# Thirty-two routed experts behind a cross attention: eight weight buffers instead of four, gate and up products in f16 halves instead of f32

## The reference

```python
x = x + xattn(layernorm(x), ctx)      # x: (4, 512, 512), ctx: (4, 1601, 512), 16 heads of 32
x = x + ffn(layernorm(x))             # 2048 tokens of 512
# ffn: router picks 4 of 32 experts a token, each expert takes at most C = 80 tokens
Xp = x[slots_token].reshape(E, C, d)
G = jnp.einsum('ecd,edi->eci', Xp, W_gate)          # 80x512 by 512x256
U = jnp.einsum('ecd,edi->eci', Xp, W_up)
Y = jnp.einsum('eci,eid->ecd', jax.nn.silu(G) * U, W_down)
Yf = Y.reshape(EC, d) * slots_w[:, None]
out = jnp.zeros((T, d), x.dtype).at[slots_token].add(Yf)
shared = jax.nn.silu(x @ shared_gate.T) * (x @ shared_up.T) @ shared_down.T
```

## Time and profile before

| | us |
|---|---|
| median of 3 runs | 1368.89 |
| the profiled execution | 1375.18 |
| its span, first to last instruction | 1373.3 |
| mean granted clock of TensorE | 0.964 |
| first part, until the second begins | 953.8 |
| first turn of gathered rows | 1152.15 |
| first scatter issued | 1165.01 |
| last scatter issued | 1366.42 |

### The profile page before, as it was taken

The page is one execution under the profiler, slowest core; times in us unless marked ns, Lnnn a source line. Parts: engine busy times, 40 slices in busy tenths (PEclk is TensorE's granted clock), DMA queues, the critical chain, the costliest instruction groups (busy, mean ns, idle before and its releaser), DMA issues. The chain is left out here.

```text
span 1373.3 us, 22309 instructions
## 1 busy us (share of the span) xinstructions
PE 1226.1 (89%) x9044; PEld 459.1 (33%) x9044; DVE 886.2 (65%) x1169; ACT 668.2 (49%) x910; POOL 184.1 (13%) x299
## 2 busy tenths in 40 slices
PE   4988999999899899989989998995798959989986
PEld 2542222444222245422224441221443423333332
DVE  6765878777587877767788766896667732222221
ACT  4546996345798534488853449882211101111111
POOL 0210000132000013200001320000200001333332
PEclk9999999999999999999999999997899989999997
DMA  7200000222000112200011122011620103989893
GB/s 276 88 23 17 2 2 10 83 70 70 24 1 1 58 41 64 93 1 1 2 69 32 62 77 94 9 55 44 257 100 3 39 1 108 308 281 321 278 289 76
DMA packets 38389, 117.82 MB, mean 86 GB/s; under 512 B 6544, under 2 KB 6800, under 8 KB 33040
## 3 DMA queue, kind: packets, MB, share of 16 engines
q1 hardware_dynamic: 33168, 105.60, 21.8%
q0 software_dynamic: 5120, 10.82, 3.7%
HBM read 95.67 MB, written 20.73 MB: 85 GB/s over the span
## 5 line engine op out<-in xcount | busy, mean ns | idle before, releaser
L567 ACT ACTIVATE work<-ps 128x1024 f32<-128x1024 f32 (+1 forms) x416 | 403.1, 1021 | 50.0 <-PE ps L1040 47.4
L1046 PE MATMUL ps<-work,vals 128*32 128x512 f32 (+2 forms) x1664 | 221.0, 604 | 1.1 <-ACT work L567 0.8
L863 PE MATMUL ps<-wts,work 128*128 128x512 f16 x864 | 203.1, 387 | 14.6 <-DVE work L596 14.6
L1040 PE MATMUL ps<-quer,keys 32*128 32x512 f16 x2496 | 171.8, 377 | 26.9 <-ACT work L567 9.3
L779 DVE TENSOR_TENSOR work<-work 128x2048 f32<-128x2048 f32 x64 | 146.6, 2291 | 5.9
L779 DVE TENSOR_TENSOR attn<-attn,work 128x2048 f32<-128x2048 f32 x64 | 146.6, 2290 | 5.3
L863 PE MATMUL ps<-wts,hl 128*128 128x512 f16 x480 | 116.6, 396 | 22.3 <-DVE hl L596 22.3
L863 PEld LDWEIGHTS ps<-wts,work 128*128 128x128 f16 x864 | 83.2, 99 | 115.1 <-DVE work L596 14.8
L1040 PEld LDWEIGHTS ps<-quer,keys 32*128 32x128 f16 x2496 | 46.2, 92 | 217.4 <-ACT work L567 192.0
L1816 PE MATMUL f_ps<-wring,xgt 128*80 128x512 f32 x256 | 116.5, 598 | 0.0
L1398 ACT ACTIVATE yf<-f_ps,wc 80x512 f32<-80x512 f32 x32 | 21.9, 683 | 174.7 <-PE f_ps L1831 168.2
(11 more groups left out here) (216 smaller groups left out, 1507.2 us busy)
## 6 DMA issues: line engine op xcount, KB each, us to landing
wring<-in_wx SPq DMA_DIRECT2D x32, 1536.0 KB, 8.1
raw<-in_ctx SPq DMA_DIRECT2D x52, 256.0 KB, 2.9
work<-in_x SPq DMA_DIRECT2D x4, 1024.0 KB, 5.4
table<-nums SPq DMA_DIRECT2D x16, 256.0 KB, 2.1
out<-x1s SPq DMA_DIRECT2D x16, 256.0 KB
work<-in_x SPq DMA_DIRECT2D x12, 256.0 KB, 4.3
x<-work SPq DMA_DIRECT2D x12, 256.0 KB, 2.0
x2t_rows<-nums SPq DMA_DIRECT2D x12, 256.0 KB, 2.4
```

What stands on the lines that cost most here:

```text
L567: act.activation(prob[0:rows, s % PROBS, 2 * half:2 * half + 2, :], ps[0:rows, 2 * pair:2 * pair + 2, :], ACT.Exp, scale=SCALE).then_inc(a ...
L863: mm = pe.matmul(out, lhs(a, c)[:, cols], wts[:, w, z, c * D:(c + 1) * D], start=(k == 0), stop=(k == len(steps) - 1))
L1040: mm = pe.matmul(ps[:, 2 * pair + h % 2, :], k[h * HD:(h + 1) * HD, :], q[h * HD:(h + 1) * HD, :], start=(e == 0), stop=(e == len(terms) - 1))
L1046: return pe.matmul(ps[h * HD:(h + 1) * HD, NUM, :], vals[a:z, ORDER[n], g * P + h * HD:g * P + (h + 1) * HD], prob[a:z, s % PROBS, h, :], ...
```

## The change

- `wring` has eight buffers of one expert's weights, spread over SBUF. Six are loaded early in the second part (experts 0, 1, 2, 4, 5, then 3), 7 and 6 during the shared expert. Gathered rows keep four buffers.
- The gate and up weights of an expert are split into f16 halves in `wsplit` (two buffers): ACT writes the high half (`weight_high`, 128x2048), DVE the low half (`weight_low`). The gathered rows are split too (`rows_high` on ACT, `rows_low` on DVE). `gate_up_rows` is then 12 f16 matmuls of 512 columns. The down product stays in f32. The copy of the turned hidden rows moves from DVE to ACT (`hidden_copy`), and the copy of the routing weight (`wc`) is gone.
- The loops of the experts are written out.
- To make room: `x2t` of batches 0 and 1 is loaded at the start of the second part, the residual rows of batches 0 to 2 share one buffer (`x1_block`), loaded batch after batch once the results of the one before are stored, and small tiles move.
- In the attention, `text_part` takes 128 columns in each of the steps 6 to 9 instead of 256 in steps 6 and 8.
- Several semaphores are merged (`d_link`, `p_link`), with the same number of waits.

```diff
 BIG = 1000.0
-RING = 4
+RING = 8
+GATHERS = 4
...
-        self.x2t = [at(f"x2t{i}", o * KB_, [P, QT, 2, NC, P], F16) for i, o in enumerate((8, 16, 48, 56))]
-        self.x1s = [at(f"x1s{i}", o * KB_, [P, 4, D], F32) for i, o in enumerate((74, 82, 90, 100))]
+        self.x2t = [at(f"x2t{i}", o * KB_, [P, QT, 2, NC, P], F16) for i, o in enumerate((48, 56, 64, 76))]
+        self.x1_last = at("x1_last", 8 * KB_, [P, QT, D], F32)
+        self.x1_block = at("x1_block", 190 * KB_, [P, QT, D], F32)
...
-        self.wring = at("wring", 132 * KB_, [P, RING, 3 * 2 * D], F32)
...
+        self.wring = [at(f"wring{i}", o * KB_, [P, 3 * 2 * D], F32)
+                      for i, o in enumerate((132, 144, 156, 168, 84, 96, 64, 48))]
+        self.wsplit = [at(f"wsplit{i}", (24 + 8 * i) * KB_, [P, 2, NC * D], F16) for i in range(2)]
...
-                for t in range(2):
-                    sp.wait_ge(f_wlo, 3 * p + 2 + t)
-                    load_turned(t)
-                sp.wait_ge(s_xt, 32 * (p + 1))
...
-                        if g > 0 and n in (6, 8):
+                        if g > 0 and 6 <= n < 10:
                             if n == 6:
                                 pe.wait_ge(a_sum, added(bb, g - 1, ADDS - 1))
-                            at = 0 if n == 6 else HALF
-                            mm = text_part(g - 1, at, at + HALF)
-                            if n == 8:
+                            at = (n - 6) * P
+                            mm = text_part(g - 1, at, at + P)
+                            if n == 9:
                                 mm.then_inc(a_den, 1)
...
+            def load_turned(b):
+                sp.dma_start(x2t[b][:, :, :, :, :].rearrange("p j a c k -> p j (a c k)"),
+                             x2_dram[b * L:(b + 1) * L, :].rearrange("(j p) n -> p j n", p=P)).then_inc(s_x2[min(b, 1)], 16)
+
+            def load_expert(n):
+                sp.dma_start(wring[n % RING][:, :], d["wx"][n]).then_inc(s_ring[n % RING], 16)
+
             sp.dma_start(x1t[:, :, :], d["x"][(B - 1) * L:B * L, :].rearrange("(j p) n -> p j n", p=P)).then_inc(s_xr, 16)
+            load_turned(0)
             sp.dma_start(rraw[:, :], d["rw"]).then_inc(s_r, 16)
             sp.dma_start(ebias[:, :], d["ebias"].partition_broadcast(P)).then_inc(s_r, 16)
-            sp.dma_start(x2t[2][:, :, :, :, :].rearrange("p j a c k -> p j (a c k)"),
-                         x2_dram[2 * L:3 * L, :].rearrange("(j p) n -> p j n", p=P)).then_inc(s_x2, 16)
-            for e in range(RING - 1):
-                sp.dma_start(wring[:, e, :], d["wx"][e]).then_inc(s_ring[e], 16)
+            load_turned(1)
+            load_turned(2)
+            for n in (0, 1, 2, 4, 5):
+                load_expert(n)
             sp.wait_ge(t_sel, NG)
-            sp.dma_start(wring[:, RING - 1, :], d["wx"][RING - 1]).then_inc(s_ring[RING - 1], 16)
+            load_expert(3)
             for j in range(QT):
                 sp.wait_ge(n_norm, j + 1)
                 sp.dma_start(table[(LB + j) * P:(LB + j + 1) * P, 0:D], xn[j]).then_inc(s_tab, 16)
-            for k in range(B - 1):
-                sp.dma_start(x1s[k][:, :, :], x1_dram[k * L:(k + 1) * L, :].rearrange("(j p) n -> p j n", p=P)).then_inc(
+
+            def load_rows(k):
+                upto(sp, s_o, 16 * QT * k)
+                sp.dma_start(x1b[:, :, :], x1_dram[k * L:(k + 1) * L, :].rearrange("(j p) n -> p j n", p=P)).then_inc(
                     s_xl, 16)
 
             def results(k):
                 for q in range(QT):
                     j = k * QT + q
                     sp.wait_ge(f_ac, j + 1)
-                    sp.dma_start(out[j * P:(j + 1) * P, :], x1s[k][:, q, :]).then_inc(s_o, 16)
-
+                    sp.dma_start(out[j * P:(j + 1) * P, :], (x1b if k < B - 1 else x1t)[:, q, :]).then_inc(s_o, 16)
+
+            load_rows(0)
             results(0)
+            load_rows(1)
             sp.wait_ge(e_wv, 1)
             sp.dma_start(table[0:T, D:TROW].rearrange("(j p) n -> p j n", p=P), rt[5][:, :, :]).then_inc(s_wt, 16)
             results(1)
+            load_rows(2)
+            sp.wait_ge(f_gu, 2 * NI)
+            load_expert(7)
+            sp.wait_ge(f_gu, 3 * NI)
+            load_expert(6)
+            results(2)
             sp.wait_ge(e_ar, 1)
             sp.dma_start(ia[:, :], arow_sb.rearrange("a (s e) -> a s e", e=E)).then_inc(s_ia, 16)
-            results(2)
             results(3)
-            with sp.Fori(0, E // RING - 1) as o:
-                for k in range(RING):
-                    sp.wait_ge(m_y, o * RING + k + 3)
-                    sp.dma_start(wring[:, k, :], d["wx"][bass.ds((o + 1) * RING + k, 1)].rearrange("a p n -> (a p) n")).then_inc(s_ring[k], 16)
+            for n in range(RING, E):
+                sp.wait_ge(m_y, n - RING + 1)
+                load_expert(n)
...
-            pool.wait_ge(f_gu, 2 * NI)
-
             def gather(n):
...
+                pool.indirect_dma_start(out=xg[n % GATHERS][:, :], out_offset=None, in_=table[:, :],
+                                        in_offset=bass.IndirectOffsetOnAxis(ap=idx[:, n:n + 1], axis=0)).then_inc(
+                    s_g[n % GATHERS], 16)
 
             def scatter(n):
...
+                pool.wait_ge(m_yf, n + 1)
+                pool.indirect_dma_start(out=out[:, :], out_offset=bass.IndirectOffsetOnAxis(ap=idx[:, n:n + 1], axis=0),
+                                        in_=yf[n % 2][:, :], in_offset=None, compute_op=ALU.add).then_inc(s_sc, 16)
+
+            for n in range(GATHERS):
                 gather(n)
             pool.wait_ge(s_o, 16 * NT)
-            for n in range(1, E + 1):
-                if n > 1:
-                    pool.wait_ge(s_sc, (n - 1) * 16)
+            for n in range(E):
+                upto(pool, s_sc, 16 * n)
                 scatter(n)
-                if n + RING <= E:
-
-                    pool.wait_ge(m_xt, n)
-                    pool.wait_ge(m_w, n + 1)
-                    gather(n + RING)
+                if n + GATHERS < E:
+                    gather(n + GATHERS)
...
-            def expert(n, u):
-                act.wait_ge(m_gu, n)
-                act.wait_ge(m_t, n)
-                act.activation(eg[:, :], ps[0:CAP, 7 if u % 2 == 0 else 0, 0:I], ACT.Tanh, scale=0.5).then_inc(m_e, 1)
-                act.wait_ge(m_y, n + 2)
-                act.wait_ge(m_w, n + 1)
-                if not isinstance(n, int):
-                    act.wait_ge(s_sc, n * 16 - 32)
-                act.activation(yf[u % 2][:, :], ps[0:CAP, 2 + u % 2, :], ACT.Copy, scale=wc[u][:, 0:1]).then_inc(m_yf, 1)
-
...
+            def weight_high(n):
+                act.wait_ge(s_ring[n % RING], 16 * (n // RING + 1))
+                if n < 2:
+                    act.wait_ge(f_gu, 4 * NI)
+                else:
+                    act.wait_ge(m_gu, n - 1)
+                act.activation(wsplit[n % 2][:, 0, :], wring[n % RING][:, 0:NC * D], ACT.Copy, scale=WS).then_inc(m_wh, 1)
+
+            def rows_high(n):
+                act.wait_ge(m_xt, n + 1)
+                upto(act, m_gu, n - 1)
+                act.copy(xgt[n % 2][:, 0, :, :].rearrange("p c s -> p (c s)"), ps[:, 6, 0:NC * CAP]).then_inc(m_xh, 1)
+
+            def expert_tanh(n):
+                act.wait_ge(m_gu, n + 1)
+                upto(act, m_h, n)
+                act.activation(eg[:, :], ps[0:CAP, 7 if n % 2 == 0 else 0, 0:I], ACT.Tanh, scale=0.5 / WS).then_inc(m_e, 1)
+
+            def hidden_copy(n):
+                act.wait_ge(m_ht, n + 1)
+                upto(act, m_y, n - 1)
+                act.copy(ht[n % 2][:, :, :].rearrange("p c s -> p (c s)"), ps[:, 1, 0:2 * CAP]).then_inc(m_hc, 1)
+
+            def weighted(n):
+                act.wait_ge(m_y, n + 1)
+                upto(act, s_sc, 16 * (n - 1))
+                act.activation(yf[n % 2][:, :], ps[0:CAP, 2 + n % 2, :], ACT.Copy,
+                               scale=xg[n % GATHERS][:, D + n:D + n + 1]).then_inc(m_yf, 1)
+
+            for n in range(2):
+                weight_high(n)
+            for n in range(2):
+                rows_high(n)
+            expert_tanh(0)
+            for n in range(E):
+                if n + 2 < E:
+                    weight_high(n + 2)
+                hidden_copy(n)
+                if n + 1 < E:
+                    expert_tanh(n + 1)
+                if n + 2 < E:
+                    rows_high(n + 2)
+                weighted(n)
...
-
-            def hidden(n, u):
-                gu = ps[0:CAP, 7 if u % 2 == 0 else 0, :]
-                dve.wait_ge(m_e, n)
-                dve.wait_ge(m_ht, n)
-                dve.scalar_tensor_tensor(hh[:, :], eg[:, :], 1.0, gu[:, 0:I], ALU.add, ALU.mult).then_inc(m_t, 1)
-                dve.wait_ge(m_t, n + 1)
-                dve.scalar_tensor_tensor(hh[:, :], hh[:, :], 0.5, gu[:, I:2 * I], ALU.mult, ALU.mult).then_inc(m_h, 1)
-                dve.wait_ge(m_ht, n + 1)
```

(61 more changed lines are left out.)

## The result

The changed kernel takes 1403.99 us in the median (four runs, 1400.33 to 1407.98), the kernel before 1368.64 us beside it (1367.94 to 1371.42): 1.0243 times as long, 95% interval 1.022 to 1.0266. It is 35 us slower, where 8 us less were forecast, and it lies above the range. The profiled execution took 1406.58 us, with a span of 1404.8 us.

A forecast was written before the change was run, and what follows sets the result against it. While loads run, POOL's serial chain of scatter, landing, next scatter was taken as the bound, PE close behind. Terms -1.4, -7.7, +4.6, -3.6 sum to -8.1 us from 1368.9: 1361 us, own range 1354 to 1367, 8-in-10 range 1347 to 1377.

The forecast's parts named there:

- Experts while loads run: 24 scatter intervals beside weight loads: still 6.42 us each, 154.1 us instead of 155.5, so -1.4 us.
- Rival B: Routed experts: weight_low on DVE holds POOL's scatter issue, 0.41 us an expert, 12.7 us, giving 1373.5 us; 15%.
- the chain of scatters: POOL, experts while loads run: each scatter waits for the landing of the last; keeps all its parts, 6.42 us an interval.
- Rival C: PE in the experts: its clock falls to 1.2 GHz after every fourth expert, 12 us, giving 1373 us; 10%.
- Rival A: Experts while loads run: the scatter chain shortens and DMA bounds at 5.92 us an interval, giving 1349 us; 15%.
- Experts after the loads: Last seven scatter intervals: 5.45 us each, 38.2 us instead of 45.9, so -7.7 us.
- the loop of `wsplit`: Experts: two wsplit buffers and ACT's order close a loop over two experts, 10.9 us, or 5.45 us an expert.
- Start of the experts: From the last residual to the first experts: two weight_low delay the first product; +4.6 us in all.
- Attention: Text parts of 128 columns at 0.35 us each cut ACT's idle time in 12 groups by 0.3 us: -3.6 us.
- rival D: Attention: text parts cost 0.54 us whatever their width, +5 instead of -3.6, giving 1369.5 us; 10%.
- Edits at nothing: x2t loads, shared residual buffer, merged semaphores, written-out loops, smaller wc transfers: no effect, x2t at 0 to +1 us.

The follow-up runs named there:

- e9: The changed kernel with five buffers for gathered rows instead of four, nothing else: 1361.9 us, 0.9955 of the kernel before.
- e3: The changed kernel without the f16 split, gate and up as four f32 matmuls, four gathered-row buffers: 1361.63 us, 0.9932 of the kernel before.
- e1: The changed kernel with the second input of weight_low taken from PSUM, low half not right: 1374.88 us, 1.0032 of the kernel before.
- e6: The changed kernel with eight buffers for gathered rows, weight_low untouched: 1365.08 us, 0.9971 of the kernel before.
- e8: The changed kernel with weight_low in four operations of 512 columns and eight gathered-row buffers: 1364.09 us, 0.9951 of the kernel before.
- e11: As e12, but the loads of experts 8 to 31 are released four experts later: 1359.99 us, 0.9929 of the kernel before.
- e5: The kernel before with the attention's text parts in quarters and nothing else: 1366.47 us, 0.9974 of the kernel before.
- e7: The changed kernel with the f32 product instead of the f16 split and eight gathered-row buffers: 1351.25 us, 0.9867 of the kernel before.
- e12: The same kernel as e7, run again on another chip: 1357.62 us, 0.9898 of the kernel before.

## Why the prediction was wrong

- **Experts while loads run (-1.4 us): the step that failed.** "The chain itself keeps all its parts" left out the loop in which the gather stands: four `xg` buffers, a turn two experts ahead of the down product, a gather behind every scatter. From rows that were at hand it could have been added up: scatter 1.43, gap 0.30, gather 0.92, landing some 4 us more (4.8 from the start of the issue to landing in the median of before), turn 0.44, down 1.94, `yf` and hand-overs 1.5, so 10.5 us for two experts against 12.8 us of two scatter intervals. It had 2.3 us of slack, and the earlier trace rows already showed it used up now and then; I read those rows for the price of the clock alone. With a held issue (+1.46), a landing 6.4 us behind the issue's end (+2.4), a slower turn (0.80 us, +0.4) and a down product at 1.2 GHz (+1.7) this estimate comes to 16.5 us; the loop takes 16.25. Measured: 191.09 us for the 24 intervals, not 154.1. With the loop opened the same f16 code takes 154.7 (e9), and the f32 product 154.2 (e3): the forecast of the chain was right where the chain was the bound.
- **Rival B** had the hold right, and its place and its price wrong. It put a held issue into the chain of scatters, at 0.41 us an expert by chance meetings, 12.7 us. Held in the gather loop they cost 29 us (after beside e1), because the meetings weren't by chance: the loop locks the gather onto `weight_low`, 18 times in 24. What they cost in the chain of scatters, where the rival had put them, no run measures while loads run; in the tail it is nothing that shows (e6 beside e8). Of the prediction's words "the two wait for each other" and "the one issued first blocks the other", one side only showed: POOL waited for a `weight_low` that had started, but DVE kept 2.29 us where a gather had started first (e9, 1217.73), and took 2.34 where a scatter followed it by 0.02 us.
- **Rival C** (clock) came as a consequence: 0.87 in the stretch, since PE idles for gathers, and its price lies inside the loop.
- **Rival A** (DMA as the bound, 5.92 us an interval) showed nowhere; no version got under 6.39 us an interval while loads ran (e11).
- **Experts after the loads (-7.7 us):** measured -7.4, 38.49 us beside 38.2 forecast. That it fits so well is luck. Most of the difference is owed to the execution of before: the same expert code took 45.88 us there and 40.24 in e5. I carried the difference and ought to have asked where the 6.3 us over the median lay. And the changed kernel still waits for gathers in its tail; with the gathers in time the tail takes 33.7 to 33.9 us (e6, e9). The pace itself was sized about right: in e9 four turns of `weight_high` take 5.29 us each, where 5.45 was forecast for the loop of `wsplit`, and PE is busy 12.50 of 13 us meanwhile:

```profile
1309.71 1.90 ACT L1412 ACTIVATE wsplit<-wring 128x2048 f16<-128x2048 f32 x1
...
1330.86 1.90 ACT L1412 ACTIVATE wsplit<-wring 128x2048 f16<-128x2048 f32 x1
```

```profile
1318.00:1331.00 13.00, 12.50 (x53) 5.75 (x52) 8.64 (x12) 7.87 (x14) 8.59 (x5) 1.00 0.32 57
```

  The tail comes out shorter than seven such turns because in the last intervals no gate and up product is left to make; the last scatters of e9 follow each other after 4.1 and 4.2 us.
- **Start of the experts (+4.6 us):** right. After the last `residual` (ends 1151.99) the first product starts 5.5 us later, 5.7 forecast, and two products take 6.77 us, 6.7 forecast:

```profile
1151.30 0.69 DVE L1513 SCALAR_TENSOR_TENSOR x_last<-f_ps,x_last 128x512 f32<-128x512 f32 x1 [1.90 <-PE f_ps L1755]
...
1151.91 4.48 DVE L1675 SCALAR_TENSOR_TENSOR wsplit<-wring,wsplit 128x2048 f16<-128x2048 f32 x2
...
1156.94 0.77 PE L1847 MATMUL f_ps<-identf,xg 80*128 80x80 f32 x4 [5.40 <-DVE xgt L1680]
1157.50 6.77 PE L1709 MATMUL f_ps<-wsplit,xgt 128*80 128x512 f16 x24
```

  From the last exponential to the first scatter the seven f16 versions take 233.2 to 234.9 us, and e3, e5, e7, e11 and e12 with the f32 product 228.6 to 229.4. The means are 4.8 us apart, 0.35% of the time. The versions with the f32 product and all the rest of the change (e3, e7, e12) are ahead of the best f16 one by 0.2 to 0.8%.
- **Attention (-3.6 us):** the size of a part (0.35 forecast, 0.33 measured) and the gain in the groups (4 batches at 1.15, -4.6) were right, and rival D, 0.54 us whatever the width, falls; 0.5, 1.3 and 1.3 us came back in the three phases between batches through the granted clock, which I hadn't counted, and the first batch began 0.8 us earlier. On its own the edit is worth 0.26%, with an interval that touches none.
- **Edits at nothing:** right together; with e3 they and the quarters stand at 0.9932. They weren't tried one by one.

Without the failed step the sum came out near: the same change with one more `xg` buffer comes to 0.9955, 6 us less, where 8 were forecast. Part of that is chance, since the term for the tail rested on the one execution of before, and the two values of the projection phases move a run by as much as the whole sum.

## What to carry to other kernels

For every ring of buffers, add up the loop that it closes, from the issue that fills it to the issue that fills it again, over the number of steps that it spans, and compare it with the pace. A term that is "kept" by a change can still go, if its slack was 2 us over two steps. When an engine gets a new operation, look at when it runs relative to the issues of the other engine: here engines released by one event met in nearly every turn of the loop (the changed kernel), or in none while loads ran (e9).

## What the runs showed of the hardware

- A DVE operation with both inputs in SBUF (128x2048, 2.29 us) holds the issue of an indirect DMA on POOL that starts while it runs: gather 0.92 to 2.38 us, scatter 1.43 to 3.51 us. A held gather ends 0.80 us after DVE's operation, a held scatter 1.3 us after it, wherever in the operation it started (18 gathers and 11 scatters of the changed kernel). DVE isn't slowed. With one input in PSUM nothing is held (925 and 1425 ns).
- An issue that starts ahead of the operation isn't lengthened, though it ends behind its start (e9, 1217.73 and 1218.33: 0.92 us). Nor was the scatter at 1174.51 in the changed kernel, which started 0.02 us behind it: 1.44 us, and DVE's operation took 2.34.
- Gathers that close the loop land late: in the changed kernel 6.4 us after the end of the held issue (1274.78 to 1281.18), in e1 5.7 to 6.9 us after the end of an issue that wasn't held. So it isn't the hold that delays the landing. Whether the load that `down_rows` releases at about the same time does wasn't tried.
- In the projection phases the traces of programs with the same first part show two values of the granted clock, 0.99 and 0.96, 3 us a phase apart, and one run shows both (e12: 124.3, 124.5 and 121.0 us between the batches). The kernel before lies between them (0.97).
